# Low halves of the weights on VectorE in place of GpSimd, in an attention block with an expert layer

## What is computed

```python
def block(x, Wq, Wk, Wv, Wo, W_base, b_base, W_router, b_router, lora_A, lora_B):   # x: 2 x 512 x 512
    q = heads(x @ Wq, 32); k = heads(x @ Wk, 8); v = heads(x @ Wv, 8)               # heads of 128
    k, v = repeat(k, 4), repeat(v, 4)
    probs = softmax(causal(q @ k.T * 128 ** -0.5))
    x = layernorm(x + concat(probs @ v) @ Wo)
    w = sparsemax(x @ W_router.T + b_router)                                        # 8 experts
    h = einsum('bsd,edr->bser', x, lora_A)                                          # rank 16
    return layernorm(x + x @ W_base.T + b_base + einsum('bser,bse,ero->bso', h, w, lora_B))
```

## Time and profile before

| | us |
|---|---|
| median of three runs | 689.89 (688.49 to 691.88) |
| the profiled execution, its own time | 687.37 |
| its span, first to last instruction | 685.3 |
| TensorE busy | 662.2 |
| VectorE busy | 543.8 |
| ScalarE busy | 412.8 |
| GpSimd busy | 279.7 |

### The profile page before, as it was taken

The page is one execution under the profiler, slowest core; times in us unless marked ns, Lnnn a source line. Parts: engine busy times, 40 slices in busy tenths (PEclk is TensorE's granted clock), DMA queues, the critical chain, the costliest instruction groups (busy, mean ns, idle before and its releaser), DMA issues.

```text
span 685.3 us, 11442 instructions
## 1 busy us (share of the span) xinstructions
PE 662.2 (97%) x3606; PEld 354.1 (52%) x3606; DVE 543.8 (79%) x1525; ACT 412.8 (60%) x1072; POOL 279.7 (41%) x424
## 2 busy tenths in 40 slices
PE   6798999999999999999999999999999999999996
PEld 3364545455554555454555555454555545445675
DVE  4899889876897679767888779767878776899774
ACT  1677566667647765667556764667656764766232
POOL 1576972167105661258004751248014550161132
PEclk9999999999999999999999999999999999999999
DMA  9347347363924256343924366444724335544411
GB/s 291 118 133 167 62 104 181 60 95 61 231 55 93 48 133 159 74 78 87 224 49 77 62 157 121 78 78 95 183 47 77 61 64 108 115 101 75 80 47 61
DMA packets 200780, 71.81 MB, mean 105 GB/s; under 512 B 169744, under 2 KB 192784, under 8 KB 200720
## 3 DMA queue, kind: packets, MB, share of 16 engines
q1 hardware_dynamic: 199376, 70.04, 46.7%
q10 hardware_dynamic: 1344, 1.05, 0.6%
HBM read 27.02 MB, written 2.10 MB: 42 GB/s over the span
## 4 chain that ended last, share of the span: by engine, by line
PE 83%; DVE 7%; DMA 3%; POOL 3%; issue 2%; SPq 1%; ACT 1%; POOLq 0%; DVEq 0%; ACTq 0%
PE bank L1128 21%; PE bank L1079 19%; PE bank L1118 13%; PE bank L1103 11%; PE bank L1091 4%; PE bank L1059 3%; PE bank L1160 3%; DMA pT<-p 2%; PE bank L1072 2%; DVE pr L929 2%; PE bank L1062 2%; DVE p L947 1%; POOL raw L678 1%; SPq L627 1%; PE bank L1171 1%
## 5 line engine op out<-in xcount | busy, mean ns | idle before, releaser
L678 POOL TENSOR_SCALAR raw<-raw,scale_of 128x512 f32<-128x512 f32 x76 | 121.0, 1593 | 162.0 <-ACT wk L740 66.2
L781 ACT ACTIVATE pr<-pr,mx 128x96 f32<-128x96 f32 (+15 forms) x256 | 131.4, 514 | 85.9 <-DVE mx L929 85.9
L790 ACT ACTIVATE p<-pr,ri 128x32 f16<-128x32 f32 (+15 forms) x256 | 118.8, 512 | 78.3 <-DVE ri L939 56.7
L1079 PE MATMUL bank<-xT,wq 128*128 128x512 f16 x720 | 164.4, 379 | 0.2 <-DVE v L849 0.2
L947 DVE SCALAR_TENSOR_TENSOR p<-pr,ri,p 128x256 f16<-128x256 f32 (+15 forms) x256 | 135.2, 572 | 35.2 <-ACT p L790 34.8
L929 DVE CUSTOM_DVE_ANT_0 pr<-bank,mask,back_of 128x32 f32<-128x32 f32 (+15 forms) x256 | 124.6, 494 | 43.3 <-PE bank L1103 42.8
L1103 PE MATMUL bank<-kT,qT 128*128 128x32 f16 (+15 forms) x768 | 124.4, 279 | 5.0 <-DVE qT L843 3.7
L1118 PE MATMUL bank<-pT,v 128*128 128x512 f16 x480 | 123.3, 379 | 3.0 <-DMA pT<-p 2.9
L1079 PEld LDWEIGHTS bank<-xT,wq 128*128 128x128 f16 x720 | 70.3, 98 | 82.2 <-DVE v L849 0.6
L691 POOL MEMSET p<- 128x64 f16 (+2 forms) x192 | 34.3, 206 | 161.8 <-DMA pT<-p 161.8
L1103 PEld LDWEIGHTS bank<-kT,qT 128*128 128x128 f16 x768 | 67.1, 98 | 64.2 <-issue 5.3
(11 more groups left out here) (121 smaller groups left out, 738.8 us busy)
## 6 DMA issues: line engine op xcount, KB each, us to landing
raw<-in_wo SPq DMA_DIRECT2D x32, 256.0 KB, 3.7
raw<-in_wq SPq DMA_DIRECT2D x30, 256.0 KB, 3.9
raw<-in_wk SPq DMA_DIRECT2D x8, 256.0 KB, 3.1
raw<-in_wv SPq DMA_DIRECT2D x8, 256.0 KB, 5.2
y<-in_x SPq DMA_DIRECT2D x1, 2048.0 KB, 13.2
pT<-p SPq DMA_TRANSPOSE x128, 3.7
out<-y SPq DMA_DIRECT2D x8, 256.0 KB, 2.0
pT<-in_xT SPq DMA_DIRECT2D x6, 256.0 KB, 7.7
```

Source lines behind the costliest of these rows:

```text
L678: eng.tensor_scalar(raw_of(name, key), raw_of(name, key), scale[0], None, ALU.mult).then_inc(sems["scaled"], 1)
L781: eng.activation(pr[:, t % 2, h, 0:w], pr[:, t % 2, h, 0:w], ACT.Exp, bias=mx[:, k:k + 1], scale=-1.0, accum_out=rs[:, k:k + 1]).then_inc( ...
L790: eng.activation(halves_of_probs(t, h)[0], pr[:, t % 2, h, 0:group(t, h)[1]], ACT.Copy, scale=ri[:, 1, k:k + 1]).then_inc(sems["p_hi"], 1)
L1079: made = eng.matmul(out, wq[:, g % 2, w, h, c * 128:(c + 1) * 128], xT[:, x, c, b * 512:(b + 1) * 512], start=c == 0 and w + x == 0, stop= ...
```

## The change

The function `late_low` picks every weight piece of a group above the first (`key[0] > 0`). Their step still writes `hi` on ScalarE, but no longer issues anything on GpSimd or makes the low half at once. The low half becomes a step of its own, `("low", piece)`, which `evicted` holds back like those of `K` and `Q`: it goes behind the next score step, or ahead of the first step that reads it, a product or the next fetch into its slot. VectorE makes it with the one operation that it has for the pieces of `ON_DVE`. These are 69 pieces: 7 `wk`, 28 `wq`, 28 `wo`, 6 `wv`. The rest of the list keeps its order.

```diff
@@ reads()
-    return [("O_lo", key[0])] if name == "W" else []
+    if name == "W":
+        return [("O_lo", key[0]), ("low", "wo", key[0] // NI // B, key[1])]
+    if name == "K":
+        return [("low", "wk", key[0] // B)]
+    if name == "Q":
+        return [("low", "wq", key[0] // B, key[1])]
+    if name == "Vp":
+        return [("low", "wv", key[0], k) for k in range(2)]
+    if name == "fetch":
+        last = {"lb": ("wk", G - 1), "wb": ("wq", G - 1, key[-1])}.get(key[0], (key[0], *([key[1] - 1, *key[2:]] if len(key) > 1 else ())))
+        return [("low", "wv", G // 2 - 1, k) for k in range(2)] if key[0] == "wra" else [("low", *last)]
+    return []
@@ evicted()
+        if name == "low":
             given.add((name, *key))
...
             held = []
+        elif late_low(name, key):
+            held.append(("low", name, *key))
@@
+def late_low(name, key):
+
+    return name in ("wq", "wk", "wo", "wv") and key[0] > 0
+
+
 def on_dve(name, key):
 
-    return (name, *key) in ON_DVE
+    return late_low(name, key) or (name, *key) in ON_DVE
@@ VectorE
-                if name in PIECES and on_dve(name, key):
+                if name in PIECES and on_dve(name, key) and not late_low(name, key) or name == "low":
+                    if name == "low":
+                        name, *key = key
+                        key = tuple(key)
                     hi, lo = halves(name, key)
```

More of the change, by code:

```diff
@@ L42, in evicted @@
         if name[-3:] == "_lo":
+            given.add((name, *key))
+        if name == "low":
             given.add((name, *key))
@@ L386, in post_ln_block @@
                 count("hi", name, *key)
-                count("lo_dve" if on_dve(name, tuple(key)) else "lo_pool", name, *key)
+                if not late_low(name, tuple(key)):
+                    count("lo_dve" if on_dve(name, tuple(key)) else "lo_pool", name, *key)
                 if not on_dve(name, tuple(key)):
                     count("scaled", name, *key)
+            elif name == "low":
+                count("lo_dve", *key)
             elif name == "most":
```

## The result

Over 11 runs each the changed kernel takes 686.56 us in the median and the kernel before 688.63: a ratio of 0.9973 (95% interval 0.9962 to 0.9984). By the ratio that is 1.9 us less (the medians themselves differ by 2.07). It lies inside the range of the prediction. The interval leaves out 1, so the kernel did become a little faster, but by less than the 0.5% that the prediction took as its bound for telling a change from none. The profiled execution has a span of 684.7 us against 685.3.

What follows compares the result with a forecast made beforehand. TensorE was taken to bound the long stretch. Removing 2.25 us of transpose waits and adding 1.5 us of new waits took the 689.89 us median to 689.1 us; range 685.8 to 693.6.

Steps and rivals of the forecast that it cites:

- The bound: From 66 to 560 us: TensorE busy 492.42 of 494 us, so other engines' edits can win at most 1.6 us there.
- The three waits: TensorE's waits for transposed probabilities at 116, 421 and 562 us all go: 2.25 us less; bounds nothing and 2.25.
- VectorE gives back 24 us: VectorE's operations with two SBUF inputs and on two columns, held up by GpSimd, get 24 of 30 us back.
- if nothing comes back: Bound on VectorE's net added work, should its operations regain no time: 51 us more, against 27 expected.
- New waits of 1.5 us: TensorE waits for low halves of oT behind new VectorE operations: 1.1 us at 89 us, 0.4 at 72 us.
- Rival D: Loop from scores to transposed probabilities: VectorE becomes late for TensorE, 8.9 us of new waits, 696.5 us; chance 0.15.
- The size: Whole kernel: 0.75 us less than the 689.89 us median of three runs, giving 689.1 us.
- mechanism A: Whole kernel: transpose waits go and new oT waits come, 689.1 us, own range 687.3 to 691; chance 0.50.
- rival C: New operations find room everywhere, TensorE loses nothing, small waits go too, at most a microsecond at the end: 686.6; chance 0.15.

Runs made afterwards that it cites:

- only_wo7: The kernel before, with only the four wo pieces of the last group moved to VectorE; 688.68 us, ratio to before 1.0010.
- not_wo7: The changed kernel, but the four wo pieces of the last group stay on GpSimd; 687.30 us, ratio to before 0.9983.
- both_moves: Changed kernel with the lb and wra fetches behind the transposes of t = 56, 57 and three low halves at 87 us held one more score step; 686.46 us.
- pool_reads: The changed kernel, with GpSimd still doing a multiply and subtract per moved piece on spare tiles; 707.57 us, ratio to before 1.0275.
- pool_writes: The changed kernel, with GpSimd doing five memsets per moved piece on spare tiles, which read nothing; 687.44 us, ratio to before 0.9982.
- wo_only: The kernel before, with only the 28 wo pieces moved to VectorE, the other 41 left on GpSimd; 688.92 us, ratio to before 1.0009.
- fetch_apart: The changed kernel with the fetches of lb and wra placed behind the transposes of t = 56 and 57; 686.22 us, ratio to before 0.9972.

## Why the prediction was right

**The bound.** Right: TensorE is busy for 493.14 of 494 us, and only its waits were there to win.

**The three waits.** Counted as gone, 2.25 us. Two were, and 0.41 of 0.72 stayed: 1.84 us by the brackets of this trace. By the starts of the products behind them it is 0.95, 0.31 and 0.91 us, 2.17 in all. The cause given for the one at 562 us is shown by only_wo7 and not_wo7. For 116 and 421 us the cause is less certain: in both_moves the wait at 116 us is back with 1.15 us although the pieces are gone from GpSimd, and in not_wo7 with 0.81, and it was 0.78 and 1.15 us in the two traces of before. Why it is there in some traces and not in others stays open.

**VectorE gives back 24 us.** Right in size (23.7 us) and, by pool_reads against pool_writes, right in cause. VectorE ended at 561.8 us of busy time and not at 571: 3.5 us are the other small operations, and some 6 us are overlap, since the prediction counted each new operation at its full 745 ns. The step was worth more than the prediction said: it named "if nothing comes back" only as a bound of VectorE's work, and the runs put 19.5 us of TensorE on it.

**New waits of 1.5 us.** At 72 us, where 0.4 was forecast, the bracket shows none, but the product with Wo starts 0.15 us later than before, counted from product 300: VectorE had the low half of `oT` at 72.10 us, 0.45 before the 72.55 that was computed, and TensorE starts on it at 72.24. At 89 us there are 0.32 us of idle time and a start 0.49 us later, counted in the same way, against 1.1: VectorE came to the scores at 86.60 in place of 86.99 us, since two operations ahead of it took 0.71 us and not 1.39. Both errors are of one kind: the relief was counted in the sum over the kernel, and not at the place. Another 0.20 us came at 105 us, where none was forecast: 0.84 us in this part, against 1.5. The wait at 582 us was not foreseen; it took 0.82 us.

**Rival D** was given 0.15. Half of the argument against it did not hold: 97 us of VectorE's idle time do not absorb 51 us of work by themselves. In pool_reads, taken together, nothing comes back: VectorE is busy for 53.6 us more than before the change, and the steady stretch is 19.1 us longer, far above the 8.9 us of new waits that D was priced at. The other half, the 24 us back, is what kept D away: the change stayed on the right side of the edge because it gives back half of what it adds. The edge lies near the changed kernel's 84% busy here, but the share is no measure of it: in wo_only a wait for VectorE appeared with 401.47 of 494 us busy.

**The size.** -0.75 us was forecast from the trace; the steady stretch of one trace gives -0.5 to -1.3, and the medians -1.9 (interval -2.6 to -1.1). What the medians have beyond that is not placed. That the net is near is partly luck. Against the first trace of before, 2.17 us removed less 0.84 and 0.82 us of new waits gives -0.51; the first new part was overrated by 0.7 us, and the wait at 582 us, not in the sum, made up for it. The forecast of 689.1 us for the median was 2.5 us too high. 1.3 us of that is the base: the three runs that it started from had a median of 689.89, and all 11 have 688.63. The measured 686.56 lies below the 687.3 to 691 that the prediction gave for its own mechanism A, and at the 686.6 of rival C; but C's mechanism, no new wait at all, did not happen. The stated range held because it was wide enough for C and half of D.

## What to carry to other kernels

When work moves between GpSimd and VectorE, price what the two do to each other first: a GpSimd operation that reads SBUF holds up VectorE's operations with two SBUF inputs, and here half of the moved work came back that way. Measure how far an in-order engine is from its edge by doubling the suspected work in a probe: idle time in sum is no measure, since it is made of waits in a loop with other engines. A wait removed ahead of the bounding engine is often met again a few steps later; compare the start times of the same product in both traces to see where the time was won and lost.

## What the hardware showed unexpectedly

With only 16% of its time idle in the long stretch, VectorE cost TensorE 0.6 us for each microsecond added. And in the first 66 us the granted clock differed between executions: 0.95 in the changed kernel (the row of the section on the result) and 1.00 before. In that trace the products of 256 columns from 31 to 37 us follow each other at 0.213 us and not at 0.109, which is the 1.2 GHz level. Before that TensorE had waited 1.91 us up to 27.61 us; before the change it had waited 1.66 us up to 27.93 us, and its clock stayed. TensorE went from 0.36 us ahead to 1.48 us behind by 37 us and was level again by 63 us, since three waits had shrunk or gone by then (0.36 us at 48, 0.54 at 60 and 0.68 at 63 us). Such a difference belongs to neither kernel: both_moves has 1.00 there, and fetch_apart, with the same first steps, 0.95.
